# A fused state-space, attention-branch and quantised-FFN kernel: layer norm, W_in and the convolution are taken through the 64-column first layer as on-chip 66-row products, each filled up to 128 rows with zeros

## The reference, cut to what matters

```
# 1  first state-space layer, N = 64 states (the "first layer")
conv  = conv_b + sum_k x_pad[:, k:k+L] * conv_w[k]   # the kernel gets conv_w as V_TAP
proj  = conv @ Wp + bp ;  B = softplus(proj[:, :64]) ; C = tanh(proj[:, 64:]) ; u = x @ Ws + bs
state = decay * state + B * u ;  y0 = C * state * dt          # 64 columns
x1    = y0 @ Wo + bo                                          # 64 -> 512
# 2  second state-space layer (Mamba-like), 1024 channels, 16 states
xn    = (x1 - mean(x1)) * rsqrt(var(x1) + eps) * ln_g + ln_b  # layer norm over 512
x_br, z = split(xn @ W_in)                                    # 512 -> 2 x 1024
xc    = causal convolution of x_br over time, 4 taps per channel, + conv_b
xb    = silu(xc)
B, C  = xb @ W_b, xb @ W_c ;  delta = softplus(xb @ W_delta + b_delta)
h     = exp(delta * A) * h + delta * B * xb                   # 1024 x 16 states, over time
out   = ((sum_n h * C + xb * Dp) * silu(z)) @ W_out + x1
# 3, 4  adapter factors from cond_1024, then a 512 -> 2048 -> 512 feed-forward with quantised weights and activations
```

## Time and profile before

| | |
|---|---|
| median of three runs | 3088.01 us |
| the profiled execution, its own time | 3081.28 us |
| span of its trace | 3079.5 us |
| VectorE (DVE) busy | 2829.8 us, 92% of the span |
| TensorE (PE) busy | 2536.5 us, 82% |
| ScalarE (ACT) busy | 1899.1 us, 62% |
| GpSimd (POOL) busy | 1585.3 us, 51% |
| mean granted TensorE clock | 0.91 |

### The profile page before, as it was taken

How to read it: one execution, slowest core, us unless ns; L and a number is a source line. 1 busy time by engine, 2 the same in 40 slices (tenths; PEclk the granted TensorE clock), 3 DMA queues, 4 the chain that set the end, 5 groups by cost and what they waited for, 6 DMA issues and landing times. The chain is left out here.

```text
span 3079.5 us, 40037 instructions
## 1 busy us (share of the span) xinstructions
PE 2536.5 (82%) x11852; PEld 1726.5 (56%) x11852; DVE 2829.8 (92%) x4347; ACT 1899.1 (62%) x3495; POOL 1585.3 (51%) x1318
## 2 busy tenths in 40 slices
PE   7788888888888888888888787878787887699997
PEld 5566566656556555656566556656565633244443
DVE  2899999999999999999999999999999993688887
ACT  3657575757575757575757575757575743455554
POOL 0456565656565656565656565656565661122221
PEclk8788998999999999899989998999899898799999
DMA  4102020202020202010201010101010442111110
GB/s 168 48 1 69 1 69 1 70 1 69 1 70 1 69 1 70 1 66 4 67 5 66 4 67 4 66 4 67 4 66 4 195 165 83 59 62 61 61 62 24
DMA packets 44540, 152.27 MB, mean 49 GB/s; under 512 B 5141, under 2 KB 6037, under 8 KB 41246
## 3 DMA queue, kind: packets, MB, share of 16 engines
q1 hardware_dynamic: 44318, 149.63, 13.8%
HBM read 132.24 MB, written 17.37 MB: 49 GB/s over the span
## 5 line engine op out<-in xcount | busy, mean ns | idle before, releaser
L748 DVE TENSOR_TENSOR_SCAN ring<-a_ps,carry,ring 128x256 f32<-128x256 f32 x2048 | 1361.6, 725 | 0.0
L571 ACT ACTIVATE a_ps<-delta,nA 128x256 f32<-128x256 f32 x2048 | 853.8, 464 | 707.6 <-DVE ring L748 693.1
L378 POOL TENSOR_TENSOR ring<-ring,Cbc 128x1024 f32<-128x1024 f32 x512 | 1215.3, 2374 | 44.2
L912 PE MATMUL yT_ps<-ident,ring 128*128 128x128 f32 x4096 | 600.2, 296 | 321.0 <-POOL ring L378 307.4
L912 PEld LDWEIGHTS yT_ps<-ident,ring 128*128 128x128 f32 x4096 | 509.5, 153 | 413.0 <-POOL ring L378 356.8
L373 POOL TENSOR_TENSOR carry<-ring,half 128x4 f32<-128x4 f32 x512 | 165.0, 322 | 988.7 <-DVE ring L748 988.7
L738 DVE TENSOR_TENSOR ring<-u_ps,Bbc 128x1024 f32<-128x1024 f32 x512 | 618.2, 1210 | 17.3 <-PE yT_ps L912 9.7
L880 PE MATMUL work<-xb,big 128*128 128x256 f32 x2048 | 487.9, 392 | 24.2 <-ACT zs L450 24.2
L880 PEld LDWEIGHTS work<-xb,big 128*128 128x128 f32 x2048 | 393.2, 198 | 80.5 <-ACT zs L450 28.6
L674 DVE SCALAR_TENSOR_TENSOR xb<-xbr,V,xb 128x256 f32<-128x256 f32 x384 | 288.1, 815 | 0.0
L859 PE MATMUL work<-big,xT 128*128 128x512 f32 x512 | 269.4, 676 | 0.0
(11 more groups left out here) (165 smaller groups left out, 2762.6 us busy)
## 6 DMA issues: line engine op xcount, KB each, us to landing
Bbc<-bc_rows SPq DMA_DIRECT2D x64, 512.0 KB, 4.4
Cbc<-bc_rows SPq DMA_DIRECT2D x64, 512.0 KB, 3.6
xT<-in_xT SPq DMA_DIRECT2D x16, 514.0 KB, 4.8
x_rows<-x2row SPq DMA_DIRECT2D x32, 256.0 KB, 2.0
big<-in_f_w SPq DMA_DIRECT2D x2, 4096.0 KB, 20.0
xp<-x_rows SPq DMA_DIRECT2D x32, 256.0 KB, 2.7
xx<-in_x SPq DMA_DIRECT2D x32, 256.0 KB, 3.0
out_rows<-orow SPq DMA_DIRECT2D x32, 256.0 KB, 2.0
```

The costliest lines, as they stand in the source:

```text
L378: nc.gpsimd.tensor_tensor(h, h, Cbc[:, G * g:G * g + G, :], ALU.mult).then_inc(s_hc, 1)
L571: r = nc.scalar.activation(a_ps[q % 2][:, i, :], delta[:, par, dt, :], ACT.Exp, scale=nA[:, dt, s:s + 1])
L748: r = dve.tensor_tensor_scan(ring[:, q % RING, i, :], a_ps[q % 2][:, i, :], ring[:, q % RING, i, :], carry[:, par, dt, s:s + 1], ALU.mult, ...
L912: r = pe.matmul(yT_ps[:, tt, :], ring[:, q % RING, i, P * tt:P * tt + P], ident[:, :], is_transpose=True, start=False, stop=(g == NG - 1 a ...
```

## The change

Before the first block, VectorE centres Wo over its 512 columns, TensorE transposes it, and `WoTg` holds it times `ln_g`, with `ln_b` as the 66th row. `make_m` multiplies it with W_in: 32 small products for x, 8 of 512 columns for z. VectorE scales the x part by the four taps (`mx_scale`), TensorE transposes it back (`turn_m`), and ScalarE copies both into `big[0]`, over W_in, as `Mx` (4 taps) and `Mz`. In each step y0 is turned, scaled by the layer norm's factor, turned back (`turn_y0`, `y0scale`, `turn_back`, `y0back`) and kept in `y0s` with three columns of history. `x` is then 4 products a channel group as before, but one per tap and with `y0s` shifted by the tap; `z` is one product instead of four. `x1copy`, `norm`, `turn`, `stats2`, `hist` and `conv` go, and `xcopy` writes once. The statistics read x1 from PSUM. Rows 66 to 127 of `y0s`, and of Wo and y0, are zeros, so that every product has 128 rows. `xT` has its own memory and is loaded at the start of a step. `y0k` lies in `big[0]`, so the feed-forward weights are loaded after the last product that reads it.

```diff
-        Wo = sb("Wo", [N0 + 1, D])
+        Wo = sb("Wo", [P, D])
-        xbr_buf = sb("xbr", [P, 4 * (T + 3)])
+        ln_full = sb("lnbuf", [P, 2 * 2 * T])
+        Mx = big[0][:, 0:4 * DI].rearrange("p (k c) -> p k c", k=4)
+        Mz = big[0][:, 4 * DI:5 * DI]
+        y0k = big[0][:, 6 * DI:6 * DI + 2 * T].rearrange("p (b t) -> p b t", b=2)
+        y0r = sb("y0r", [P, NT, NY])
+        y0s = sb("y0s", [P, 2, T + 3])
...
@@ SyncE @@
                 if last:
                     sp.wait_ge(s_scan, NQ * k)
                     sp.dma_start(chunk[0], c2_w1).then_inc(s_cw1, 16)
                     sp.wait_ge(s_gate, ND * k)
                     sp.dma_start(chunk[1], c2_w2[0]).then_inc(s_chunk[0], 16)
-                    sp.wait_ge(full[BANK["DL3"]], jobs_before("DL3", k - 1) + 1)
-                    for i, w in enumerate((f_w1, f_w2)):
-                        sp.dma_start(big[i][:, :], w).then_inc(s_big[i], 16)
                 if back:
...
                 if last:
+                    sp.wait_ge(full[BANK["WOUT1"]], jobs_before("WOUT1", k) + 1)
+                    for i, w in enumerate((f_w1, f_w2)):
+                        sp.dma_start(big[i][:, :], w).then_inc(s_big[i], 16)
                     def keep_row(c):
...
@@ ScalarE @@
-                def x1copy(tt): ...
-                def norm(): ...
-                def turn(j): ...
+                def y0scale():
+                    ps = take("YT")
+                    act.wait_ge(s_rstd, n + 1)
                     for tt in range(NT):
+                        r = nc.scalar.activation(y0r[:, tt, 0:N0 + 1], ps[:, NY * tt:NY * tt + N0 + 1], ACT.Copy,
                                                  scale=nrm[:, 1, tt:tt + 1])
+                    r.then_inc(free[BANK["YT"]], 1)
+                def y0back():
+                    ps = take("YB")
+                    nc.scalar.activation(y0s[0:NY, fp, 0:3], y0s[0:NY, fp, T:T + 3], ACT.Copy).then_inc(s_yh, 1)
+                    act.wait_ge(s_yh, n + 1)
+                    nc.scalar.activation(y0s[0:NY, fp, 3:T + 3], ps[0:NY, 0:T], ACT.Copy).then_inc(free[BANK["YB"]], 1)
...
-                next_plan = {5: [prj], 6: [prj_ln], 8: [lambda: x1copy(0)], 9: [lambda: x1copy(1)], 11: [norm],
-                             12: [lambda: turn(0), lambda: turn(1)], 14: [lambda: xcopy(0)],
+                next_plan = {5: [prj], 6: [prj_ln], 10: [y0scale], 11: [y0back], 14: [lambda: xcopy(0)],
...
-                back_plan = {6: [lambda: gT(ND // 2 - 1, fp)], 9: [lambda: wout(0)], 12: [lambda: wout(1)]}
+                back_plan = {6: [lambda: gT(ND // 2 - 1, fp)], 9: [lambda: wout(0)], 11: [lambda: wout(1)]}
+                    if isinstance(k, int) and k == -1 and q == 13:
+                        mz_copy()
+                        mx_copy()
@@ VectorE @@
-                def stats2(): ...
-                def hist(j): ...
-                def conv(j): ...
+                def mx_scale(): ...                       # 32 tensor_scalar of 128 x 66, step -1 only
-                next_plan = {4: [gates0], 5: [scan0], 8: [stats], 9: [stats2], 11: [keep_y0],
-                             12: [lambda: hist(0), lambda: hist(1)], 14: [lambda: conv(0), lambda: hist(2)],
-                             15: [lambda: conv(1), lambda: hist(3)], 16: [lambda: conv(2)], 17: [lambda: conv(3)],
+                next_plan = {4: [gates0], 5: [scan0], 8: [stats], 13: [keep_y0],
@@ TensorE @@
+                def turn_y0():
+                    ps = give("YT")
+                    for tt in range(NT):
+                        r = pe.transpose(ps[:, NY * tt:NY * tt + NY], y0[0:NY, P * tt:P * tt + P], ident[0:NY, 0:NY])
+                    r.then_inc(full[BANK["YT"]], 1)
+                def turn_back():
+                    ps = give("YB")
+                    pe.wait_ge(free[BANK["YT"]], jobs_before("YT", k) + 1)
...
+                def make_m():
+                    weights(3)
+                    pe.wait_ge(s_wog, 2)
+                    for half in range(2):
+                        for m in range(4 * half, 4 * half + 4):
+                            for d in range(KD):
+                                r = pe.matmul(abank[half][:, NY * (m % 4):NY * (m % 4) + NY], Win[:, d, P * m:P * m + P],
+                                              WoTg[:, d, :], start=(d == 0), stop=(d == KD - 1))
+                        r.then_inc(s_mxt, 1)
+                    for c in range(2):
+                        for d in range(KD):
+                            r = pe.matmul(abank[2 + c][0:NY, :], WoTg[:, d, :],
+                                          Win[:, d, DI + 512 * c:DI + 512 * c + 512],
+                                          start=(d == 0), stop=(d == KD - 1))
+                        r.then_inc(s_mz, 1)
...
-                    for d in range(KD):
-                        r = pe.matmul(ps[:, T * m:T * m + T], Win[:, d, c:c + P], xnT[:, d, :],
-                                      start=(d == 0), stop=(d == KD - 1))
+                    for tap in range(4):
+                        r = pe.matmul(ps[:, T * m:T * m + T], Mx[:, tap, c:c + P], y0s[:, fp, tap:tap + T],
+                                      start=(tap == 0), stop=(tap == 3))
...
+                def z(j):
+                    ps = give(f"Z{j}")
+                    tt, c = j // 2, 512 * (j % 2)
+                    pe.matmul(ps[:, :], y0s[:, fp, 3 + P * tt:3 + P * tt + P], Mz[:, c:c + 512],
+                              start=True, stop=True).then_inc(full[BANK[f"Z{j}"]], 1)
...
-                        7: [("b", wout, 1, 0)], 8: [("b", wout, 1, 1)], 9: [("b", wout, 1, 2)], 10: [("n", turn)],
+                        7: [("b", wout, 1, 0)], 8: [("b", wout, 1, 1)], 9: [("b", wout, 1, 2), ("n", turn_y0)],
+                        10: [("n", turn_back)],
```

More of the change, by code:

```diff
@@ L28 @@
 RANK = 8
+NY = N0 + 2
 EPS = 1e-5
@@ L147, in scan_phase @@
         yT_ps = pb("yT_ps", [P, NT, P])
+        abank = [a_ps[i // 2][:, 2 * (i % 2):2 * (i % 2) + 2, :].rearrange("p a b -> p (a b)") for i in range(4)]
         u_full = pb("u_ps", [P, 512])
@@ L244, in step @@
                 last = isinstance(k, int) and k == NBLK - 1
+                if front and not (isinstance(k, int) and k == NBLK - 2):
+                    sp.wait_ge(full[BANK["PRJ"]], jobs_before("PRJ", k) + 1)
+                    sp.dma_start(xT[:, :, :], xT_in[bass.ds(n + 1, 1)].rearrange("a p k t -> (a p) k t"))\
+                        .then_inc(s_xload, 16)
                 if last:
@@ L445, in zcopy, with mx_copy @@
+                def mx_copy():
+                    for m in range(ND):
+                        act.wait_ge(s_mxp, m + 1)
+                        nc.scalar.activation(Mx[0:NY, :, P * m:P * m + P],
+                                             abank[2 + m % 2][0:NY, :].rearrange("p (k c) -> p k c", k=4), ACT.Copy)\
+                            .then_inc(s_mxc, 1)
                 def zcopy(j):
@@ L637, in stats @@
                     for tt in range(NT):
-                        dve.wait_ge(free[BANK[f"WO{tt}"]], jobs_before(f"WO{tt}", k) + 1)
-                        dve.bn_stats(stat[:, tt, :], xn[:, tt, :]).then_inc(s_stat, 1)
-                    dve.wait_ge(s_stat, 4 * n + 2)
+                        job = f"WO{tt}"
+                        dve.wait_ge(full[BANK[job]], jobs_before(job, k) + 1)
+                        dve.bn_stats(stat[:, tt, :], work[BANK[job]][:, :]).then_inc(free[BANK[job]], 1)
+                    dve.wait_ge(free[BANK["WO1"]], jobs_before("WO1", k) + 1)
                     dve.memset(mark[:, :], 0.0)
@@ L760, in step @@
                 for q in range(NQ):
+                    if isinstance(k, int) and k == -1 and q == 12:
+                        mx_scale()
                     for job in (scan_plan.get(q, []) if scan else []):
@@ new lines, in turn_m @@
+                def turn_m():
+                    for m in range(ND):
+                        pe.wait_ge(s_mxs, m + 1)
+                        if m < 2:
+                            pe.wait_ge(s_mzc, m + 1)
+                        else:
+                            pe.wait_ge(s_mxc, m - 1)
+                        for tap in range(4):
+                            r = pe.transpose(abank[2 + m % 2][0:NY, P * tap:P * tap + P], MTk[:, m, tap, :], ident[:, :])
+                        r.then_inc(s_mxp, 1)
@@ L842, in x @@
                 def x(j, m):
                     if j == 0 and m == 0:
-                        weights(3)
-                        for t in range(2):
-                            pe.wait_ge(free[BANK[f"XNT{t}"]], jobs_before(f"XNT{t}", k) + 1)
+                        pe.wait_ge(free[BANK["YB"]], jobs_before("YB", k) + 1)
+                        if isinstance(k, int) and k == -1:
+                            pe.wait_ge(s_mxc, ND)
                     ps = work[BANK[f"XB{j}"]] if m else give(f"XB{j}")
@@ L853, in x @@
                         r.then_inc(full[BANK[f"XB{j}"]], 1)
-                def z(j, part):
```

(16 more changed lines are left out.)

166 lines of the change are left out of this document (72 added, 94 removed).

## The result

| | before | after |
|---|---|---|
| median | 3086.01 us (3083.62 to 3090.0) | 2952.44 us (2949.14 to 2955.52) |
| profiled execution, its own time | 3081.28 us | 2949.14 us |
| span | 3079.5 us | 2947.1 us |
| mean granted TensorE clock | 0.91 | 0.903 |

The changed kernel is faster: ratio 0.9566 with a 95% interval of 0.9549 to 0.9582. The sign was forecast, the size was not. 2952 us lies 112 us above the forecast and 60 above the end of its range.

What follows compares the result with a forecast made beforehand. VectorE was taken to set the pace of steps 0 to 14. 3081.3 - 286.5 (VectorE work) + 9 (hand-offs) + 12.3 (start) + 19 (end) = 2835.1 us, put at a median of 2840; range 2812 to 2892.

Steps and rivals of the forecast that it cites:

- the work taken from VectorE: Steps 0 to 14: four convolution jobs, history copies and `stats2` leave VectorE, 19.1 us a step, 286.5 us in all.
- The walk through the slots: Slots 8 to 17 of a step, timed from slot 8's start, to find late hand-offs; W_out products end at 9.1.
- The hand-off term: Steps 0 to 14: late hand-offs between engines cost 0.6 us a step, 9 us in all.
- The first place: Slot 10: ScalarE's `y0scale` waits for `turn_y0` ahead of the exponentials VectorE needs; 0.3 us a step.
- rival A: Slots 10 and 14: late hand-offs cost 3 to 6 us a step, giving 2871 to 2916 us; chance 0.11.
- the second place: Slots 11 to 14: `x` on TensorE in shortened VectorE slots makes `turn_states` late; about 0.3 us a step.
- Rival B: Slots 15 to 18: TensorE's clock falls, VectorE loses 1 to 4 us a step, 2850 to 2895 us; chance 0.10.
- Rival D: Steps: TensorE at half clock becomes the bound, slower than before, about 3250 to near 3980 us; chance 0.02.
- first guard: Argument against TensorE becoming the bound: padded products keep their 128 rows, in shapes that ran at full clock.
- The start: Before the first scan: `make_m` and preparing Wo add 22.2 us, shorter work saves 7.2 and 2.7; +12.3 us.
- The end: Step 15: a `c2_w2` piece queues behind 8 MB of feed-forward weights, TensorE stands still; +19 us.
- the signs that the prediction named against itself: VectorE waiting over 1 us for ScalarE (slot 10) or `turn_states` (slots 15-17, 20-24), or no long wait in step 15.

Runs made afterwards that it cites:

- early statistics: Against the kernel after the change: the first of the two bn_stats moved from VectorE's slot 8 to slot 6; 2875.51 us, ratio 0.933.

## Why the prediction was wrong

- **What bounds the kernel, and the work taken from VectorE: right.** The step was put at 155.0 - 19.1 = 135.9 us, which leaves 135.2 of VectorE work. The step shown of the kernel after has 134.8.
- **"Nothing is added to VectorE there: `stats` reads PSUM instead of SBUF at the same length": this step failed.** The length was right (0.67 and 0.70 us; before, both together 1.26). What it left out is that an instruction which reads a PSUM bank also gives it back. With `x1copy` gone, the release of bank 0 between the two halves passed from the engine that runs ahead to the one that sets the pace. The walk through the slots took W_out's end, 1070.27, time 9.1, from the old step, in which TensorE did not wait at the second x1 product. In the kernel after, `turn_y0` stands at 1024.64, 14.3 us after slot 8 begins at 1010.34; with the bank given back early it stands at 8.9.
- **The hand-off term, 0.6 us a step: mis-sized.** In the mean of steps 0 to 14 it is 143.45 - 135.9 = 7.5 us. The first place named was the right one, and its mechanism (exponentials behind `y0scale`) is rival A's. That rival priced 3 to 6 us from the slack alone and ended at 2916, since it too let TensorE come on time. With the bank given back early the step is 138.2, 2.3 over 135.9: 0.6 is the `nrm` instruction (1.83 us, before 1.24), and 1.7 are hand-offs, still three times the term, mostly at the second place, `x` in slots 11 to 14.
- **The second place: right in kind.** VectorE waits 1.38 us for `yT_ps` at 1047.32, in slot 15, and up to 2.95 in other steps.
- **Rival B, the clock: it came true in kind, and small.** The B and C products, 3.64 us in every step before, take 5.0 to 6.6 us in 10 of the 15 steps of the kernel after. In six of these VectorE waits 1.1 to 1.2 us just behind them, in slot 21, 6.7 us in all; the rival had priced 1 to 4 us in every step. The clock is low in slots 8 and 9 too, where it stretches the catching up; its share there was not separated from the wait that comes with it.
- **Rival D, TensorE as the bound: it did not come, and its first guard was what mattered.** The clock of the step shown is 0.90, far from 0.69. "The padded products keep their 128 rows" proved to be the point. Without the zeros the time is 3087.61 us, no faster than before. The profile of before could not price it, for all its long runs have 128 rows.
- **The start, +12.3 foreseen, +22.1 measured.** `make_m` took 13.76 and 8.79 us instead of 11 and 7.2, because TensorE came to it at the lower clock level, so the first `x` product stands at 59.92 and not at 55.9. Preparing Wo took what it should: the second x1 product ends 3.5 us later than before, foreseen 3.4. The B and C products (5.30 us, before 3.61) and the second group of delta products (15.77, before 14.08) each lost 1.7 us at the lower clock behind waits of 3.23 us, which the prediction did not have. The last z was to save 2.7 us and saved nothing: the delta products behind it wait for ScalarE's z copy (3.23 us, before 0.69), so the shorter z only made that wait longer.
- **The end, +19: right.** Measured +21.9, of it 19.7 the queue (158.1 less 138.4), and the wait in the trace is 18.31 us. The other 2.2 us were not followed up.

Of the signs that the prediction named against itself, three stand in this step of the kernel after: VectorE waits 3.08 us for ScalarE in slot 10, and 1.38 and 1.10 us for `turn_states` in slots 15 and 21.

By size, the sum of 2835.1 is short by 101 us in the steps, 10 at the start and 3 at the end. Taking back the bank, the queue and the order at the start brings the kernel to 2840.42 us, where the forecast of 2840 had put it. That is a coincidence of parts, for the last of these edits also beats the start that was predicted.

What stays open: the last 1.7 us of hand-offs in a step, what the closing instruction of the statistics would give if it stood clear of GpSimd's product, and whether a second PSUM bank for x1's second half would do as well as the early statistics. None of these was tried.

## What to carry to other kernels

When a change deletes a copy out of a shared buffer, ask who gives the buffer back now, and when that engine gets there. An engine that sets the pace is the worst one to hold a buffer others need, even if its own work grows by nothing. And in an engine's in-order list, put what waits for a late partner behind what the pace-setter needs.

## What the runs showed of the hardware

- In slots 11 to 14 the rows of the products, with their columns unchanged, decided whether TensorE's granted clock came back. After the same wait, 32 records of 128x256 took 7.60 us and 32 of 66x256 took 13.86. Filling up all of these products with zeros was worth 135 us of 3088, 9.2 us a step.
- Scattered short products showed little of this: z at 66 rows 630 ns a record, at 128 rows 630; the whole kernel 7.6 us.
- The same 64 small records took 7.36 us behind other products and 13.76 us behind waits. At the start of this program the order on TensorE decided the clock at which the block ran.
- A VectorE instruction of two columns took 0.17 us when GpSimd's product of 1024 columns was over, and 1.24 (before) or 1.83 (early statistics) when it met that product. It then ended within 0.03 us of it, in all 15 steps of both kernels.
